# Attention with a mixture of experts on one core: grouping rewritten and shared with ScalarE and GpSimd, stacks of batch 0 ahead of most row stores, five unread products between the first scores

## Chip, cores, metric

One core of one Trainium2 chip. The metric is the device time of one execution in microseconds, median of several runs. One launch computes everything.

## What is computed

`x` has 8 batches of 512 tokens with 128 features, fp32. The reference, cut to what matters:

```python
xn = layernorm(x)                                   # no weights
q, k, v = xn @ Wq + bq, xn @ Wk + bk, xn @ Wv + bv  # 8 heads of 16
attn = softmax(q k^T / 4)
out = attn (v1 - lam v2)      # v1: first four heads' values, v2: last four, each used by both halves
s = (0.2 * (layernorm(out) * ln_w + ln_b)) @ Wo + bo
h = mod(int(xn[:, 0] + xn[:, 1]), 8)                # routing: experts h and h+1
f = sum over the two experts e of 0.5 * (relu(xn @ W1[e] + b1[e]) @ W2[e] + b2[e])
y = x + s * silu(f)
```

## The kernel before, in words

**Layout.** A batch is four tiles of 128 tokens, so there are 32 token tiles (`NT`). Attention takes 256 score products (`score` n, line 1289), one for each batch, head and query tile; VectorE takes the negative maximum of each (line 1049). 24 places later the same scores are made again with keys in the partitions and the maximum taken off (`exp` n, line 1314), ScalarE takes the exponential (line 787), and `pv` (line 1327) sums. To have fp32 scores from bf16 products, q and k are each split into three bf16 parts (`parts`), of which six pairs are stacked along the partitions of `qs` and `ks` by DMAs of SyncE. For batches 0 and 1 the split is done by peels: TensorE makes the projection again and subtracts the parts already there (lines 1255 and 1258), and ScalarE copies the rest out as the next part (line 774). For batch 1 the parts are in a piece of `probs`.

**Mixture.** The tokens are sorted by expert. VectorE computes h for each token (`count_groups`, lines 886 to 911): v01 = xn0 + xn1, its integer part towards zero, modulo 8; then `onehot`, `count` per expert and partition, and running sums `seen`. TensorE sums the counts over the partitions (`route` 1, lines 1359 and 1360), `make_slots` turns them into a slot for each token, `find_tokens` (lines 943 to 948) and `find_rows` (line 953) build bf16 indicator tiles, and 32 products (`invert`, line 1367) give `inverse`: which token stands in each sorted slot. GpSimd then gathers tiles of 128 sorted tokens from the DRAM copy `xn_rows` (line 650). It first waits for `inverse` and for all eight stores of that copy (line 541, SyncE). Seven extra tiles (f = 0 to 6) hold tokens at the edges between experts: `turn_tile`, `hidden`, `down`, then z (line 1167), stored by SyncE to `init_rows` (line 556). The 32 sorted tiles (f = 7 to 38) follow at one per 6.85 scores; each begins with a gather of `init_rows` (line 678) that waits for all stores of z, and VectorE adds its products to it (lines 1174, 1176).

**Order.** All engines walk one list, `schedule()`: every step has a time written by hand, the list is sorted by it, and each engine does its own kinds of steps in that order. The unit is one score; times below 0 are the head. Nothing but that order and the semaphores decides when a step runs. `ring` is three PSUM banks given in turn to transposes, projections, peels, route, invert and the expert products; a new user waits for the reader of the use three back.

**The head.** VectorE takes bn_stats of each batch as it lands (line 1005). GpSimd makes rstd = (var + eps) ** -0.5 (lines 630, 631) and shift = -mean * rstd (lines 629, 635), by groups of batches (`LN_GROUPS`); for the last group the shift is made by VectorE (line 1019). ScalarE normalises batches 0 to 3 (line 755), GpSimd 4 to 7 (line 640). TensorE waits for DVE's `count` at `route`, which stands behind all of batch 0's peels and batch 1's transpose. Both peels of each of batch 1's projections stand ahead of `invert`. ScalarE's list goes: norms, batch 0's parts, batch 1's transpose copy, norms 2 and 3 among batch 1's parts, bias copies (lines 743 to 747, which set `table_ready`, a condition of score 0), ten small loads (lines 718 to 727), the DMAs of ones (line 731), then tile 0's transpose copy (line 832). SyncE's list goes: stores of batches 0 and 1, twelve stack DMAs of batch 0 (line 532), stores of batches 2 to 7, the W2 loads (line 502, once tile 1 has landed), a store of b2, z of tile 0, then twelve stack DMAs of batch 1, stores of z, and pair loads.

## Time and profile before

| what | us |
|---|---|
| median of three runs (409.14 to 410.87) | 409.66 |
| the profiled execution | 411.52 |
| its span, first to last instruction | 409.6 |
| TensorE busy | 381.5 (93%) |
| VectorE busy | 291.8 (71%) |
| ScalarE busy | 267.5 (65%) |
| GpSimd busy | 189.3 (46%) |

The mean granted TensorE clock is 0.991 of full speed. In the profile PE is TensorE, PEld its weight loads, DVE is VectorE, ACT ScalarE, POOL GpSimd and SP SyncE; a q behind the name is the engine's queue, which issues DMAs. L12 is line 12 of the kernel. In the chain of waits each piece is what the next had to wait for.

### The profile page before, as it was taken

To read this page: it belongs to the slowest core of one execution; us is meant where nothing else is said; L and a number is where in the kernel's file an instruction comes from. 1 tells how busy PE (TensorE), PEld (TensorE's weight loads), DVE (VectorE), ACT (ScalarE), POOL (GpSimd) and SP (SyncE) were. 2 spreads that over 40 slices of the span, in tenths; PEclk is the share of its full clock that TensorE was granted. 3 is DMA by queue.
4 is the path that set the end of the run, shared out by engine and by line. 5 is a ranking of instruction groups with operands and counts; after the bars stand their busy time and mean duration, and the time that the engine had idled before them with its cause. 6 is when DMAs were issued, how large, how long until landed. Compare 5 with 4: busy or idle time off the path is not lost.

```text
span 409.6 us, 8427 instructions
## 1 busy us (share of the span) xinstructions
PE 381.5 (93%) x2576; PEld 248.3 (61%) x2576; DVE 291.8 (71%) x758; ACT 267.5 (65%) x667; POOL 189.3 (46%) x262
## 2 busy tenths in 40 slices
PE   4996989999999999999999999999999999999993
PEld 2353876565775667766665668765676667764321
DVE  7787996656686757766676767866686767866884
ACT  3581756666765776576666767676766668675783
POOL 7944203454456543565355532663573444541200
PEclk9996999999999999999999999999999999999999
DMA  7975953263216451265105640346136141216740
GB/s 263 343 230 112 242 196 91 80 206 105 79 37 191 111 195 21 79 190 168 46 27 170 189 140 18 136 121 197 48 127 216 22 169 47 81 26 213 230 159 26
DMA packets 36945, 54.75 MB, mean 134 GB/s; under 512 B 6724, under 2 KB 25141, under 8 KB 36903
## 3 DMA queue, kind: packets, MB, share of 16 engines
q1 hardware_dynamic: 31456, 46.94, 34.6%
q0 software_dynamic: 3296, 6.76, 7.8%
q10 hardware_dynamic: 2151, 0.53, 0.6%
q8 instruction: 22, 0.36, 0.4%
q14 instruction: 20, 0.16, 0.1%
HBM read 15.59 MB, written 6.75 MB: 55 GB/s over the span
## 4 chain that ended last, share of the span: by engine, by line
PE 74%; DVE 7%; DMA 5%; ACT 4%; SPq 4%; issue 4%; POOL 1%; ACTq 0%; DVEq 0%; POOLq 0%
PE ring L1393 14%; PE pv_bank L1327 13%; PE ring L1414 12%; PE score L1289 12%; PE exp L1314 10%; PE ring L1251 3%; DVE neg_max L1049 3%; DMA xs<-xn_rows,inverse 3%; SPq L532 2%; PE ring L1335 2%; PE ring L1255 1%; PE ring L1353 1%; PE ring L1276 1%; PE ring L1375 1%; PE score L1264 1%
## 5 line engine op out<-in xcount | busy, mean ns | idle before, releaser
L1049 DVE TENSOR_REDUCE neg_max<-score 128x1 f32<-128x512 f32 x256 | 169.0, 683 | 72.3 <-PE score L1289 66.7
L1289 PE MATMUL score<-ks,qs 96*128 96x512 bf16 x256 | 98.3, 386 | 6.3 <-DVE neg_max L1049 6.0
L787 ACT ACTIVATE probs<-exp 128x512 f32<-128x512 f32 x124 | 72.5, 605 | 36.3 <-PE exp L1314 32.3
L787 ACT ACTIVATE xin<-exp 128x512 f32<-128x512 f32 x120 | 69.7, 604 | 38.5 <-PE exp L1314 38.1
L1314 PE MATMUL exp<-qs,ks 99*128 99x512 bf16 x244 | 91.7, 380 | 0.1
L825 ACT ACTIVATE hT<-ring,pair 128x128 f32<-128x128 f32 x256 | 73.4, 377 | 13.0 <-PE ring L1393 11.9
L1414 PEld LDWEIGHTS ring<-w_sb,hT 128*128 128x128 f32 x568 | 73.5, 191 | 10.4 <-issue 3.5
L1414 PE MATMUL ring<-w_sb,hT 128*128 (+1 forms) x568 | 75.4, 275 | 0.9 <-ACT hT L825 0.9
L1393 PEld LDWEIGHTS ring<-xsT,pair 128*128 128x128 f32 x512 | 66.3, 191 | 14.6 <-issue 8.1
L1393 PE MATMUL ring<-xsT,pair 128*128 128x128 f32 x512 | 68.2, 276 | 1.7 <-issue 1.2
L684 POOL TENSOR_SCALAR tanh<-tanh 128x128 f32<-128x128 f32 x32 | 17.2, 536 | 95.5 <-ACT tanh L845 95.2
L1289 PEld LDWEIGHTS score<-ks,qs 96*128 96x128 bf16 x256 | 25.9, 102 | 45.3 <-DVE neg_max L1049 24.0
L650 POOL DMA_INDIRECT xs<-xn_rows,inverse x39 | 38.5, 988 | 24.3 <-issue 10.2
L678 POOL DMA_INDIRECT y_sb<-init_rows,init_row x32 | 31.2, 974 | 29.0 <-DMA init_rows<-oT 17.3
L691 POOL DMA_INDIRECT y_rows<-y_sb,inverse x32 | 34.4, 1076 | 9.0 <-POOL y_sb L685 9.0
L1327 PE MATMUL pv_bank<-xin,va 128*32 128x512 f32 x256 | 31.2, 599 | 0.8 <-ACT xin L787 0.7
L1314 PEld LDWEIGHTS exp<-qs,ks 99*128 99x128 bf16 x244 | 23.9, 98 | 12.5 <-issue 1.9
L1327 PE MATMUL pv_bank<-probs,va 128*32 128x512 f32 x256 | 31.2, 599 | 0.0
L1174 DVE SCALAR_TENSOR_TENSOR y_sb<-ring,first_expert,y_sb 128x128 f32<-128x128 f32 x32 | 11.1, 348 | 15.2 <-PE ring L1375 8.7
L1251 PE MATMUL ring<-xT,wqk 128*128 128x512 f32 x32 | 18.0, 657 | 1.3 <-ACT xT L750 1.3
L845 ACT ACTIVATE tanh<-y_sb 128x128 f32<-128x128 f32 x32 | 9.8, 305 | 11.2 <-DVE y_sb L1176 11.1
L769 ACT ACTIVATE parts<-ring,qk_bias 128x512 bf16<-128x512 f32 x14 | 9.6, 689 | 9.7 <-PE ring L1251 9.7
(198 smaller groups left out, 417.4 us busy)
## 6 DMA issues: line engine op xcount, KB each, us to landing
pair<-table SPq DMA_DIRECT2D x32, 580.0 KB
qs<-parts SPq DMA_DIRECT2D x42, 128.0 KB
ks<-parts SPq DMA_DIRECT2D x42, 128.0 KB
xin<-_attn_hidden_states_dram SPq DMA_DIRECT2D x8, 256.0 KB, 4.4
table<-in_L_ffn_W_dram SPq DMA_DIRECT2D x2, 1024.0 KB, 9.2
w_sb<-in_L_ffn_W_dram SPq DMA_DIRECT2D x8, 256.0 KB, 10.4
xn_rows<-xn SPq DMA_DIRECT2D x8, 256.0 KB, 3.0
table<-_attn_hidden_states_dram SPq DMA_DIRECT2D x8, 256.0 KB, 5.4
```

The lines of the kernel that those rows point to most:

```text
L650: pool.indirect_dma_start(xs[:, f % XS, :], None, xn_rows, bass.IndirectOffsetOnAxis(ap=inverse[:, f:f + 1], axis=0)).then_inc(tile_loaded ...
L678: pool.indirect_dma_start(y_sb[:, tile % YB, :], None, init_rows, bass.IndirectOffsetOnAxis(ap=init_row[:, tile:tile + 1], axis=0)).then_i ...
L691: pool.indirect_dma_start(y_rows, bass.IndirectOffsetOnAxis(ap=inverse[:, f:f + 1], axis=0), y_sb[:, tile % YB, :], None).then_inc(y_store ...
L787: a.activation(prob(n), exp_banks[n][:, :], ACT.Exp, scale=SCALE).then_inc(exp_done, 1)
L825: last = a.activation(hT[:, f % 2, FC * j + c, :], shared[:, c * P:(c + 1) * P], ACT.Relu, bias=bias)
L1049: v.tensor_reduce(neg_max[:, b % 2, col:col + 1], score_bank[n % 2][:, :], AX.X, ALU.max, negate=True).then_inc(max_taken, 1)
L1251: t.matmul(shared[:, :], wqk[:, i, :], xT[:, b % 2, :], start=True, stop=True).then_inc(shared_filled, 1)
L1289: t.matmul(score_bank[n % 2][:, :], qs[0:MAX_ROW, b % STK, hh, c * P:(c + 1) * P], ks[0:MAX_ROW, b % STK, hh, :], start=True, stop=True).t ...
L1314: t.matmul(exp_banks[n][:, :], ks[0:KROWS, b % STK, hh, kc * P:(kc + 1) * P], qs[0:KROWS, b % STK, hh, :], start=True, stop=True).then_inc ...
L1327: last = t.matmul(pv_bank[VW * i:VW * (i + 1), :], va[:, b % 2, kc, i, :], prob(4 * n4 + i), start=(kc == 0), stop=(kc == C - 1))
L1393: last = t.matmul(shared[:, c * P:(c + 1) * P], w1_chunk, xsT[:, f % 2, :], start=True, stop=True)
L1414: last = t.matmul(shared[:, half * D:(half + 1) * D], hT[:, f % 2, k, :], w2_chunk, start=(k % FC == 0), stop=(k % FC == FC - 1))
```

## The change

- Groups of batches: the last pair is split, (6, 7) and (7, 8). GpSimd makes no shift in the groups behind batch 3; it makes that of batches 4 to 7 at once behind the last `rstd`. VectorE's shift is gone: it adds -2 * mean to the sum of the two raw features before `rstd` is there, and multiplies by `rstd` after.
- `count_groups`: integers are read and written without casts between; `seen` is made by a scan over `onehot` shifted by one element.
- ScalarE makes the second of the two token products (`tokens`); ScalarE also normalises batch 4, and batch 2 earlier.
- `route` goes ahead of batch 0's last peel; the second peels of batch 1's two projections go behind score 1 and score 5.
- SyncE: batch 2's store goes ahead of batch 0's stacks, batch 0's last stack part behind the stores of 4, 5 and 6. The ones DMAs move from ScalarE's queue to SyncE's, ahead of W2.
- `keep_busy`: one unread product behind each of scores 2, 3 and 4 and two behind the peel that follows score 5, each 96x128 by 96x512 in bf16 into an unused bank.
- Extra tiles start one score later (`FFN_FIRST`), and small moves of tanh, `split_max` and the gathers of `init_rows` (`TANH`, `SPLIT_MAX`, `INIT_AHEAD`).

The diff, with its context cut:

```diff
-LN_GROUPS = ((0, 1), (1, 2), (2, 4), (4, 6), (6, 8))
-POOL_NORM = (4, 5, 6, 7)
+LN_GROUPS = ((0, 1), (1, 2), (2, 4), (4, 6), (6, 7), (7, 8))
+POOL_NORM = (5, 6, 7)
+LATE_SHIFT = 4
+EARLY_GROUPS = 3
 STATS_AT = (-60, -59, -58, -57, -56, -55, -54, -52)
-SHIFT_AT = (-58.5, -57.5, -55.5, -53.5, -50)
-NORM_AT = (-58, -56.4, -49.9, -47.93, -49.2, -49.1, -49, -48.95)
+SHIFT_AT = (-58.5, -57.5, -55.5, -53.5, -53.4, -50)
+NORM_AT = (-58, -56.4, -56.3, -48.61, -48.7, -48.68, -48.66, -48.63)
 FOLD_QK_AT = -57.95
-QKV_AT = (-57.9, -50, 35, 67, 99, 131, 163, 181)
+QKV_AT = (-57.9, -48.62, 35, 67, 99, 131, 163, 181)
 PROJECT_AT = ((-55.9, -55.6), (-47.95, -45.9))
-PEEL_AT = (((-55.5, -55.3), (-55.4, -55.25)), ((-45.5, -45.3), (-45.4, -45.2)))
-STACK_AT = (((-55.58, -55.45, -55.28), (-55.57, -55.35, -55.2)), ((12.1, 12.3, 12.5), (12.2, 12.4, 12.6)))
+PEEL_AT = (((-55.5, -55.3), (-55.4, -48.65)), ((-45.5, 1.5), (-45.4, 5.3)))
+STACK_AT = (((-55.58, -55.45, -55.28), (-55.57, -55.35, -48.64)), ((12.1, 12.3, 12.5), (12.2, 12.4, 12.6)))
 ROUTE_AT = (-48.8, -48.7)
-TOKENS_AT = -45
+TOKENS_AT = -45.6
 INVERT_AT = -40
-EXTRAS_AT = 5.2
-GROUPS_AT = (9.05, 10.72, 13.05, 14.05)
+EXTRAS_AT = 5.9
+GROUPS_AT = (9.05, 10.72, 12.55, 14.05)
 ONES_AT = -45.09
-FFN_FIRST = 7.6
+FFN_FIRST = 8.6
 FFN_PACE = 6.85
-TX, DX = 2.4, 3.2
+TX, DX = 3, 3.2
 PAIR_AT = (20, 21, 22)
-INIT_AHEAD = 1.5
+INIT_AHEAD = 1.67
 TT = 2
-SPLIT_MAX, TURN_MAX = 16.8, 18.9
+SPLIT_MAX, TURN_MAX = 16.5, 18.9
 FOLD_AT = 20.5
-TANH, GATE = 0.7, 1.84
+TANH, GATE = 1, 1.84
 HALVES = 2
+WARM_AT = ((2.5, 1), (3.5, 1), (4.5, 1), (5.4, 2))
...
     at(INVERT_AT, "invert")
+    for time, products in WARM_AT:
+        at(time, "keep_busy", products)
...
         sign = sb("sign", [P, NT])
-        h = sb("h", [P, NT])
+        h_i = sb("h_i", [P, NT], I32)
...
         inverse_f = cmp[:, 0:FT]
-        onehot = work[:, 512:768].rearrange("p (e t) -> p e t", e=EXP)
-        seen = work[:, 768:1024].rearrange("p (e t) -> p e t", e=EXP)
+        onehot = work[:, 511:767].rearrange("p (e t) -> p e t", e=EXP)
+        seen = work[:, 767:1023].rearrange("p (e t) -> p e t", e=EXP)
...
         token_ready = sem("token_ready")
+        in_tile_ready = sem("in_tile_ready")
...
                                          parts_of(b)[:, i, k, :]).then_inc(stacked[b % STK], 16)
+                elif kind == "ones":
+                    sp.wait_ge(dve_consts, 1)
+                    for slot_b in range(STK):
+                        sp.dma_start(ks[MAX_ROW:KROWS, slot_b, :, :],
+                                     ones_bf[:, :].unsqueeze(1).to_broadcast([PARTS, HEADS, S])).then_inc(ones_stacked, 16)
...
                     pool.wait_ge(stats_ready, end)
-                    if end < B:
+                    if first < LATE_SHIFT:
                                     ALU.pow).then_inc(rstd_ready, 1)
-                    if end < B:
+                    if first < LATE_SHIFT:
                         g.tensor_tensor(shift[:, tok], shift[:, tok], rstd[:, tok], ALU.mult).then_inc(shift_ready, 1)
+                    if end == B:
+                        late = slice(C * LATE_SHIFT, NT)
+                        pool.wait_ge(rstd_ready, len(LN_GROUPS))
+                        link(g.tensor_scalar(shift[:, late], mv[:, late, 0], -1.0, None, ALU.mult))
+                        g.tensor_tensor(shift[:, late], shift[:, late], rstd[:, late], ALU.mult).then_inc(shift_ready, 1)
+                        pool.wait_ge(shift_ready, EARLY_GROUPS + 1)
                     b = s[1]
-                    pool.wait_ge(shift_ready, 1 + [b >= end for _, end in LN_GROUPS].index(False))
...
                     act.dma_start(lnb_sb[:, :], ln_b.rearrange("(p a) -> p a", a=1)).then_inc(small_loaded, 16)
-                elif kind == "ones":
-                    act.wait_ge(dve_consts, 1)
-                    for slot_b in range(STK):
-                        act.dma_start(ks[MAX_ROW:KROWS, slot_b, :, :],
-                                     ones_bf[:, :].unsqueeze(1).to_broadcast([PARTS, HEADS, S])).then_inc(ones_stacked, 16)
...
                     a.activation(xT[:, s[1], :], shared[:, :], ACT.Copy).then_inc(xT_ready, 1)
+                elif kind == "tokens":
+                    act.wait_ge(in_tile_ready, 1)
+                    a.activation(token[:, 1, :, :, :], in_tile, ACT.Copy, scale=row_of[:, 0:1]).then_inc(token_ready, 1)
...
             v.memset(zeros, 0.0)
+            v.memset(work[:, 767:768], 0.0)
...
                 dve.wait_ge(pair_summed, 1)
+                dve.wait_ge(rstd_ready, len(LN_GROUPS))
                 link(v.tensor_tensor(v01[:, :], v01[:, :], rstd[:, :], ALU.mult))
-                dve.wait_ge(shift_ready, len(LN_GROUPS))
-                link(v.scalar_tensor_tensor(v01[:, :], shift[:, :], 2.0, v01[:, :], ALU.mult, ALU.add))
                 v.tensor_scalar(sign[:, :], v01[:, :], 0.0, 2.0, ALU.is_ge, ALU.mult)
-                link(v.tensor_copy(n_abs[:, :], whole_i))
-                link(v.tensor_tensor(over, n_abs[:, :], v_abs[:, :], ALU.is_gt))
-                link(v.tensor_tensor(n_abs[:, :], n_abs[:, :], over, ALU.subtract))
-                link(v.scalar_tensor_tensor(h[:, :], sign[:, :], -1.0, n_abs[:, :], ALU.add, ALU.mult))
-                link(v.tensor_copy(whole_i, h[:, :]))
-                link(v.tensor_scalar(whole_i, whole_i, EXP - 1, None, ALU.bitwise_and))
-                link(v.tensor_copy(h[:, :], whole_i))
-                link(v.tensor_tensor(onehot[:, :, :], h[:, :].unsqueeze(1).to_broadcast([P, EXP, NT]),
+                link(v.tensor_tensor(over, whole_i, v_abs[:, :], ALU.is_gt))
+                link(v.tensor_tensor(n_abs[:, :], whole_i, over, ALU.subtract))
+                link(v.scalar_tensor_tensor(h_i[:, :], sign[:, :], -1.0, n_abs[:, :], ALU.add, ALU.mult))
+                link(v.tensor_scalar(h_i[:, :], h_i[:, :], EXP - 1, None, ALU.bitwise_and))
+                link(v.tensor_tensor(onehot[:, :, :], h_i[:, :].unsqueeze(1).to_broadcast([P, EXP, NT]),
-                flat = work[:, 768:1024]
-                link(v.tensor_tensor_scan(flat, work[:, 512:768], zeros,
-                                          0.0, ALU.add, ALU.add))
-                v.tensor_tensor(seen[:, :, :], seen[:, :, :], onehot[:, :, :], ALU.subtract).then_inc(seen_ready, 1)
+                v.tensor_tensor_scan(work[:, 768:1024], work[:, 511:767], zeros,
+                                     0.0, ALU.add, ALU.add).then_inc(seen_ready, 1)
...
                 dve.wait_ge(slots_split, 1)
-                link(v.tensor_tensor(in_tile, by_pair(slot_tile[:, 0:NT], FT), over_pairs(columns[:, :, :], NT // 2), ALU.is_equal))
-                v.tensor_tensor(token[:, 0, :, :, :], in_tile, by_pair(ordinal[:, :], FT), ALU.mult)
-                v.tensor_scalar(token[:, 1, :, :, :], in_tile, row_of[:, 0:1], None, ALU.mult).then_inc(token_ready, 1)
+                v.tensor_tensor(in_tile, by_pair(slot_tile[:, 0:NT], FT), over_pairs(columns[:, :, :], NT // 2),
+                                ALU.is_equal).then_inc(in_tile_ready, 1)
+                dve.wait_ge(in_tile_ready, 1)
+                v.tensor_tensor(token[:, 0, :, :, :], in_tile, by_pair(ordinal[:, :], FT), ALU.mult).then_inc(token_ready, 1)
...
                         continue
-                    tok = slice(C * first, C * end)
-                    v.tensor_tensor(v01[:, :], xin[:, :, 0], xin[:, :, 1], ALU.add).then_inc(pair_summed, 1)
-                    dve.wait_ge(rstd_ready, g + 1)
+                    link(v.tensor_tensor(v01[:, :], xin[:, :, 0], xin[:, :, 1], ALU.add))
                     dve.wait_ge(stats_ready, end)
-                    v.scalar_tensor_tensor(shift[:, tok], mv[:, tok, 0], -1.0, rstd[:, tok],
-                                           ALU.mult, ALU.mult).then_inc(shift_ready, 1)
+                    v.scalar_tensor_tensor(v01[:, :], mv[:, :, 0], -2.0, v01[:, :],
+                                           ALU.mult, ALU.add).then_inc(pair_summed, 1)
...
                              ks[0:MAX_ROW, b % STK, hh, :], start=True, stop=True).then_inc(score_filled, 1)
+                elif kind == "keep_busy":
+                    for _ in range(s[1]):
+                        t.matmul(exp_bank[1][:, :], qs[0:MAX_ROW, 0, 0, 0:P], ks[0:MAX_ROW, 0, 0, :], start=True, stop=True)
...
                 elif kind == "invert":
-                    pe.wait_ge(token_ready, 1)
+                    pe.wait_ge(token_ready, 2)
```

## Rows read from the trace of the kernel before

**Rows 1.** Busy time by stretch: engines, granted clock, DMA share, GB/s.

```profile
29.00:30.00 1.00, 1.00 (x24) 0.88 (x23) 0.97 (x5) 0.78 (x2) 0.00 (x0) 1.00 0.00 0
...
34.00:35.00 1.00, 0.00 (x0) 0.00 (x0) 0.96 (x4) 0.00 (x0) 0.78 (x1) 0.50 0.42 115
...
100.00:150.00 50.00, 48.59 (x344) 33.26 (x343) 35.23 (x84) 34.24 (x87) 25.26 (x32) 1.00 0.38 116
```

**Rows 2.** Chain of waits to 75 us: start, us, what.

```profile
31.45 4.89 DMA xs<-xn_rows,inverse
...
37.93 1.71 PE ring L1393 x8
...
61.53 2.96 DMA init_rows<-oT
```

**Rows 3.** VectorE in order of time, scores: start, us, line, [idle before, releaser].

```profile
31.06 3.67 DVE L1049 TENSOR_REDUCE neg_max<-score 128x1 f32<-128x512 f32 x6
...
37.39 1.29 DVE L1049 TENSOR_REDUCE neg_max<-score 128x1 f32<-128x512 f32 x2 [1.16 <-PE score L1289]
...
40.10 1.29 DVE L1049 TENSOR_REDUCE neg_max<-score 128x1 f32<-128x512 f32 x2 [1.42 <-PE score L1289]
...
43.78 0.35 DVE L1167 SCALAR_TENSOR_TENSOR oT<-ring,uses_extra,oT 128x128 f32<-128x128 f32 x1
...
68.92 0.35 DVE L1174 SCALAR_TENSOR_TENSOR y_sb<-ring,first_expert,y_sb 128x128 f32<-128x128 f32 x1 [1.21 <-DMA y_sb<-init_rows,init_row]
```

**Rows 4.** GpSimd in order of time: powers, shift and norms.

```profile
8.14 1.04 POOL L631 TENSOR_TENSOR rstd<-var_eps,neg_half 128x4 f32<-128x4 f32 x1
...
14.60 0.20 POOL L635 TENSOR_TENSOR shift<-shift,rstd 128x8 f32<-128x8 f32 x1
...
15.21 1.67 POOL L631 TENSOR_TENSOR rstd<-var_eps,neg_half 128x8 f32<-128x8 f32 x1
...
16.87 8.19 POOL L640 TENSOR_SCALAR xn<-xin,rstd,shift 128x128 f32<-128x128 f32 x16
```

**Rows 5.** VectorE in order of time: the grouping.

```profile
16.91 0.17 DVE L1019 SCALAR_TENSOR_TENSOR shift<-mv,rstd 128x8 f32<-128x8 f32 x1 [2.00 <-POOL rstd L631]
...
17.21 0.19 DVE L892 SCALAR_TENSOR_TENSOR v<-shift,v 128x32 f32<-128x32 f32 x1
...
17.98 0.28 DVE L897 CAST n_abs<-hT 128x32 f32<-128x32 int32 x1
...
18.98 0.18 DVE L901 CAST hT<-h 128x32 int32<-128x32 f32 x1
...
21.22 0.49 DVE L911 TENSOR_TENSOR hT<-hT 128x256 f32<-128x256 f32 x1
...
26.79 0.54 DVE L948 TENSOR_SCALAR probs<-hT,row_of 128x1248 bf16<-128x1248 bf16 x1
...
27.24 2.42 DVE L953 TENSOR_TENSOR qs<-hT,grid 128x1536 bf16<-128x1536 bf16 x3
```

**Rows 6.** Costliest groups of the page: busy us, mean ns.

```profile
L787 ACT ACTIVATE probs<-exp 128x512 f32<-128x512 f32 x124 | 72.5, 605 | 36.3 <-PE exp L1314 32.3
...
L825 ACT ACTIVATE hT<-ring,pair 128x128 f32<-128x128 f32 x256 | 73.4, 377 | 13.0 <-PE ring L1393 11.9
```

**Rows 7.** ScalarE in order of time: a norm, loads issued, ones, tile copy.

```profile
21.94 1.64 ACT L755 ACTIVATE xn<-xin,shift,rstd 128x128 f32<-128x128 f32 x4
...
29.33 0.35 ACTq L718 DMA_DIRECT2D lams<-in_L_attn_lambda_q_dram  x1
...
34.46 2.46 ACTq L731 DMA_DIRECT2D ks<-ones_bf  x3
...
36.97 0.28 ACT L832 ACTIVATE xsT<-ring 128x128 f32<-128x128 f32 x1 [6.96 <-PE ring L1375]
```

**Rows 8.** TensorE in order of time: a late peel of batch 1.

```profile
27.83 1.02 PE L1255 MATMUL ring<-xT,wqk 128*128 128x512 f32 x2
```

**Rows 9.** Stores of normalised rows, line 541: time to landing.

```profile
DMA to landing us min/median/max: 2.1/3.0/8.1
```

## The prediction

> **What bounds the kernel now.** I read the stretches first. From 100 us on TensorE is busy 48.6 of 50 us [rows 1], and the stretches after it look alike until the drain. A head start won in front of that region is therefore passed on to the end unless something else sets its beginning. So the question is when the dense region begins. The chain of waits says what leads there: the grouping on VectorE, the gather of the first tile of sorted tokens (31.45 to 36.34), the products of that tile, then from 44 us SyncE issuing DMAs one after another, the last store of `init_rows` (61.53 to 64.49), its gather, and VectorE waiting 1.21 us for it at 68.92 [rows 2, 3]. The reader should see three things in it. (a) Everything up to 31.15 us is latency: `inverse` ends there and the gather's issue starts 0.3 us later. (b) TensorE is idle from 34 to 36.4 us, and its granted clock falls to 0.50, the 1.2 GHz level, as the last of six scores, with 0.2 us of idle time between each two, is through; the eight products of the first tile then take 1.71 us, and would take half of that at 2.4 GHz [rows 1, 2]. (c) VectorE waits for TensorE twice there, 1.16 us before the score maximum at 37.39 and 1.42 us before the one at 40.10 [rows 3].
>
> **The routing chain on VectorE.** It waits for `rstd` of the last group, done by GpSimd at 16.88. GpSimd is the late one: its powers follow each other. The new split makes two powers of 4 columns (1.04 us each) out of one of 8 (1.67 us), and one more var_eps (0.3 us from its start to the power's): 0.7 us longer. The two shift operations taken out of the group of batches 4 and 5 (the second 14.60 to 14.88) give back 0.6 us [rows 4]. So `rstd` comes at 16.9 to 17.1, and this edit buys nothing; I take 16.9. Behind it five dependent operations go: the shift added to v01 (0.19), three casts (0.28, 0.18, 0.18 for the one not shown) and the subtraction in `seen` (0.49), 1.32 us, with the shift's 0.08 us of start-to-start time: 1.4 us [rows 5]. Added are the wait-free -2·mean term (hidden in the 2.0 us wait for `rstd`) and nothing else. Moving the route products ahead of the last peel of batch 0 is needed for this, since that peel held TensorE until 20.85. Then the product of `in_tile` with the row number leaves VectorE: 26.79 to 27.24, another 0.45 us [rows 5]. Rows now end at 29.58, and would end at 27.7: 1.85 us earlier.
>
> **That product on ScalarE.** It has no row. The nearest: 377 ns for 128 elements with a bias per row (L825) and 605 ns for the 512 of an exp without (L787) [rows 6], about 0.6 ns per element; against the 280 ns of a tile copy (36.97) it is 0.85 [rows 7]. From a norm (0.41 us for 128 elements, 1.64 for four) 1248 elements then cost 1.1 to 1.4 us. Bounds: 0.45 us as on VectorE, and 2.5 us at twice the slope. I take 1.3: the tile copy and the exp are alike in form and differ in length alone. ScalarE also gains batch 4's norms (1.64 us) and does batch 2's earlier; by my list of its work in order it reaches the token product at 25.5 and ends it at 26.8, ahead of the last rows at 27.7. So it is hidden; at 2.5 us it would end at 28.0 and cost 0.1 to 0.3 us. GpSimd keeps 12 of 16 norms (8.19 us for 16): from about 17.5, behind the late shift, to 23.7 [rows 4].
>
> **Inversion and gather.** The two last peels of batch 1 (1.02 us of fp32 products each and one or two bf16 ones of 0.2 us behind them) leave the stretch before the inversion [rows 8], and the inversion waits for the rows alone: 28.1 instead of 30.6, `inverse` at 28.65 instead of 31.15, gather landed at 33.85 instead of 36.34 with the old 4.89 us [rows 2]. First maximum: `table_ready` comes at about 28.5 behind ScalarE's bias copies, so 29.05 instead of 31.06 [rows 3], 2.0 us.
>
> **Between the first scores.** The two peels put in take 1.3 us of TensorE each. The first delays score 2 by half a microsecond on VectorE; the rest stands in gaps of 0.2 us and in the old idle time. The five products nobody reads cost 0.22 us each, 1.1 us, all in time in which TensorE waited for maxima or the gather; with the cover gone they would cost 1.1 us. TensorE is then busy from 29 to within half a microsecond of tile 0, so I expect 1.00 granted throughout. It saves about half of the products in 36.4 to 40.6 (1.71 becomes 0.86 for tile 0) [rows 2]. With that, and hidden 0 one score later, VectorE's two waits (2.6 us [rows 3]) shrink to 0.8 us, 0.45 behind the first peel and 0.35 behind hidden 0.
>
> **ScalarE before tile 0.** The three ones DMAs (2.46 us of its queue) go to SyncE, which is idle there. But the ten small loads (29.33 to 34.46, where the ones DMAs follow) now stand ahead of the last two peels [rows 7]. They start with the third copy of batch 1, about 28.45, and end at 33.55; two copies of 0.6 us follow; tile 0 is copied at 34.75 to 35.05, instead of 36.97. So 1.9 us there, and late is not the gather but ScalarE. Counting on: maximum 8 done at 36.6, hidden 0 ends at 36.6, groups 0 at 38.4, groups 1 at 40.0, maximum 11, then z of tile 0 at 40.9 instead of 44.13 [rows 3]: 3.2 us. VectorE's own work is 3.7 us ahead there, as z now follows maximum 11.
>
> **SyncE and init_rows.** From z of tile 0 the queue runs without a gap: 12 stack DMAs, stores, pairs, until the transfer that starts at 61.53 [rows 2]. It moves rigidly by 3.2 us. The last z comes one score, a tile copy and two bias operations later (about 1.4 us), at 57.9 with VectorE's 3.7 us; SyncE reaches its store at 58.3 and still is the late one. `y_sb` is there at 65.7 instead of 68.92. Behind this TensorE's and VectorE's orders are the same. Only the tanh moves on ScalarE behind one exp or copy in 11 of 32 tiles, 0.6 us each; the tile's store and the gather two tiles on follow it a whole tile (some 9 us) ahead of their use. GpSimd's order stays. Zero; with that cover gone, 0.6 us a tile.
>
> **Sum:** 2.0 (first maximum) + 1.8 (VectorE's waits, 2.6 less 0.8) - 0.6 (a maximum of that length now ahead of z) = 3.2 us, carried on by SyncE. The profiled execution took 411.52 us (span 409.6 us), so 408.3 us; it stands 1.9 us over the median of 409.66 us, and against that median the forecast is **406.4 us**. Bounds of its own: 2.2 us if the gather or ScalarE is 1 us later, 4.2 us if they are earlier: 405.5 to 407.5.
>
> **A rule that speaks against it.** GpSimd's norms average 0.51 us (8.19 for 16) and run beside VectorE's chain [rows 4]. The Trainium skill (SBUF — State Buffer, section on its two separate sides) says that a VectorE operation with two SBUF inputs and a GpSimd operation hold a shared port pair one at a time. This trace agrees as far as the norms go: some take 0.8 us, others 0.45.
>
> **Rivals.** Port: what leaves the chain are mostly one-input casts; seven operations with two SBUF inputs stay beside the norms. If each now meets a norm at a worse moment, half of one, 0.25 us, is added: 1.7 us of the 3.2, 407.9 us. That is what the skill's rule would allow; for it speaks the spread of the norms, against it that VectorE had the same neighbour before. ScalarE: if its list before tile 0 is 1.5 us longer than counted (the token product at its upper bound, loads issued late), 1.7 us remain, 408.0 us. For it: 5.1 us of issues in a row. More: if SyncE's chain no longer leads, VectorE's 3.7 us plus the 1.2 us wait at 68.92 come through, 4.9 us at most, 404.8 us. Little: the clock falls all the same, VectorE's 1.8 us are not won, and its last z, 1.4 us later in the order, comes at 59.7 with the store's transfer at 60.4; 1.1 us is left, 408.6 us. For it: the products nobody reads fill the gaps only in part. Slower: the gather also waits for all eight stores of normalised rows. They take 3.0 us in the median and 8.1 us at worst to land [rows 9], and the one of batch 3 is now last, issued at about 25.4. Landing after 31.4 it decides; at 8.1 us it lands at 33.5, 2.1 us later than the gather's start today, TensorE cools again, and the time is 411.8 us. Against it: no DMA moves from 29 to 30 us today [rows 1], and the bytes are the same.
>
> **How the numbers follow.** Chances: forecast 0.56, port 0.08, ScalarE 0.12, more 0.12, little 0.08, slower 0.04. A measurement tells about 0.5%, 2.05 us, from no change. Faster takes the forecast, more and about half of the port and ScalarE cases: 0.78; slower 0.04; the rest, 0.18, is the same. The range takes in the forecast, the middle cases and most of more: 404.7 to 408.9 us.
>
> **What would show it.** Right: v_abs about 0.25 us behind `rstd`, `count` near 19.6, `inverse` near 28.7, granted clock 1.00 from 30 to 44 us, tile 0 copied by ScalarE near 35, z of tile 0 near 41, `y_sb` near 65.7, and the same distance from there to the end. Wrong: the clock at 0.5 before tile 0 although the products are there, the gather released by the stores, or a dense region that begins 3 us earlier and ends where it did.

## The result and the profile after

| | median, us | range, us | runs |
|---|---|---|---|
| before, in this comparison | 410.57 | 409.04 to 411.90 | 20 |
| after | 409.01 | 406.57 to 414.18 | 20 |

The ratio is 0.9965 (95%: 0.9948 to 0.9981), 0.35% or 1.4 us faster, where 3.2 us were forecast. The forecast's median, 406.4 us, lies below every one of the 20 runs of after; the fastest comes within 0.2 us of it. Of the 2.6 us between that forecast and the median, 0.9 us lie in its starting point: before's three runs had a median of 409.66 us, its twenty here one of 410.57. The rest is what has to be explained. The second thing to see is the width: the runs of before lie within 2.9 us, those of after within 7.6 us.

The profiled execution of after took 409.53 us (span 407.8, mean granted clock 0.995), 2.0 us under the 411.52 us of before's.

Stretches of after: busy time of TensorE, its weight loads, VectorE, ScalarE, GpSimd, then the granted clock, DMA share, GB/s.

```profile
29.00:30.00 1.00, 0.68 (x15) 0.53 (x12) 0.32 (x2) 1.00 (x5) 0.00 (x0) 1.00 0.18 30
34.00:35.00 1.00, 1.00 (x5) 0.39 (x4) 0.93 (x4) 0.16 (x1) 0.11 (x1) 1.00 0.24 61
...
68.00:70.00 2.00, 1.59 (x9) 0.95 (x8) 1.90 (x8) 1.27 (x3) 1.03 (x2) 0.88 0.24 25
70.00:72.00 2.00, 2.00 (x11) 1.15 (x13) 1.48 (x4) 1.00 (x5) 1.58 (x2) 0.50 0.13 39
72.00:74.00 2.00, 2.00 (x17) 0.38 (x10) 0.00 (x0) 0.31 (x2) 0.76 (x2) 0.76 0.16 41
...
100.00:150.00 50.00, 49.17 (x350) 33.92 (x348) 35.90 (x84) 34.16 (x87) 25.77 (x33) 1.00 0.39 118
```

Against [rows 1] the hole at 34 us is gone (TensorE busy 1.00 of 1, clock 1.00). But there is a new one: from 70 to 72 us the granted clock is 0.50, the 1.2 GHz level, in a place where before had none.

TensorE of after in order of time: the first bias products, then the transpose of tile 8, its eight products, and an attention step.

```profile
6.72 3.75 PE L1272 MATMUL score<-probs,ones 2*128 2x512 f32 x4 [6.72 <-DMA probs<-in_L_ffn_b_dram]
...
67.75 0.33 PE L1386 MATMUL ring<-ident,xs 128*128 128x128 f32 x1 [1.25 <-DMA xs<-xn_rows,inverse]
...
69.37 1.76 PE L1404 MATMUL ring<-xsT,pair 128*128 128x128 f32 x8
...
71.29 2.72 PE L1338 MATMUL pv_bank<-probs,va 128*32 128x512 f32 x16
```

TensorE waits 1.25 us for tile 8's gathered tokens. Before it waited 0.58 us there. Within two microseconds, while it is busy again, it runs at half the clock: by the chain (next fence) tile 8's eight products take 1.60 us where tile 0's take 0.89.

Chain of waits of after, as in [rows 2].

```profile
31.92 4.97 DMA xs<-xn_rows,inverse
...
37.50 0.89 PE ring L1404 x8
...
60.66 2.33 DMA init_rows<-oT
...
63.76 3.75 DMA y_sb<-init_rows,init_row
...
69.53 1.60 PE ring L1404 x8
```

VectorE of after in order of time, as in [rows 3, 5]; in square brackets the idle time before it and who ended it.

```profile
19.13 0.42 DVE L917 TENSOR_REDUCE count<-hT 128x8 f32<-128x256 f32 x1
...
21.09 0.17 DVE L925 TENSOR_TENSOR_SCAN group_end<-ring,hT 128x8 f32<-128x8 f32 x1 [0.88 <-PE ring L1371]
...
26.19 2.42 DVE L963 TENSOR_TENSOR qs<-hT,grid 128x1536 bf16<-128x1536 bf16 x3
...
29.92 0.18 DVE L1149 CAST inverse<-hT 128x39 int32<-128x39 f32 x1
...
30.27 1.29 DVE L1057 TENSOR_REDUCE neg_max<-score 128x1 f32<-128x512 f32 x2 [0.17 <-PE score L1297]
32.00 2.48 DVE L1057 TENSOR_REDUCE neg_max<-score 128x1 f32<-128x512 f32 x4 [0.44 <-PE score L1297]
...
36.36 1.89 DVE L1057 TENSOR_REDUCE neg_max<-score 128x1 f32<-128x512 f32 x3 [0.39 <-PE score L1297]
38.65 0.69 DVE L1057 TENSOR_REDUCE neg_max<-score 128x1 f32<-128x512 f32 x1 [0.40 <-PE score L1297]
...
42.31 0.34 DVE L1175 SCALAR_TENSOR_TENSOR oT<-ring,uses_extra,oT 128x128 f32<-128x128 f32 x1
...
67.53 0.35 DVE L1182 SCALAR_TENSOR_TENSOR y_sb<-ring,first_expert,y_sb 128x128 f32<-128x128 f32 x1 [1.86 <-DMA y_sb<-init_rows,init_row]
...
80.16 0.34 DVE L1182 SCALAR_TENSOR_TENSOR y_sb<-ring,first_expert,y_sb 128x128 f32<-128x128 f32 x1
```

The second `y_sb` of before:

```profile
79.98 0.34 DVE L1174 SCALAR_TENSOR_TENSOR y_sb<-ring,first_expert,y_sb 128x128 f32<-128x128 f32 x1
```

ScalarE of after in order of time, as in [rows 7]: the token product, the first and the last small load, tile 0's copy.

```profile
26.68 1.32 ACT L764 ACTIVATE probs<-hT,row_of 128x1248 bf16<-128x1248 bf16 x1
...
28.25 0.35 ACTq L734 DMA_DIRECT2D lams<-in_L_attn_lambda_q_dram  x1
...
33.41 1.38 ACTq L743 DMA_DIRECT2D lnb_sb<-in_L_attn_ln_b_dram  x1
...
36.08 0.28 ACT L846 ACTIVATE xsT<-ring 128x128 f32<-128x128 f32 x1
```

The steps, in us from the start, with two experiments beside them (e1 and e8, below):

| | before | forecast | after | e1 | e8 |
|---|---|---|---|---|---|
| first bias products start | 5.82 | - | 6.72 | 5.85 | 6.05 |
| `count` ends | 20.51 | 19.6 | 19.55 | 19.47 | 19.58 |
| `inverse` ends | 31.15 | 28.65 | 30.10 | 29.05 | 29.48 |
| first maximum starts | 31.06 | 29.05 | 30.27 | 28.99 | 29.55 |
| z of tile 0 ends | 44.13 | 40.9 | 42.65 | 41.63 | 41.90 |
| first `y_sb` (tile 7) | 68.92 | 65.7 | 67.53 | 66.28 | 66.04 |
| second `y_sb` (tile 8) | 79.98 | - | 80.16 | 77.34 | 77.17 |

The last row is the finding. After leads by 1.39 us at the first `y_sb` and trails by 0.18 us one tile later: between the two it takes 12.63 us, before 11.06 us. The stretch at half clock costs 1.57 us and eats the lead. From the second `y_sb` to that of the last tile it takes 291.71 us in after (until 371.87) and 293.74 us in before (until 373.72), with the granted clock at 1.00 in both. The change doesn't explain those 2.0 us: e7 below keeps before's order and takes 291.70 us for that distance. So the 2.0 us by which the profiled execution of after beats before's come from a stretch in which the change gains nothing. That is one more reason not to read the change's worth from one pair of executions.

### The profile page after: what moved, and what is told of

It is laid out like the page before. It is cut to its first block, busy times and chain, and to the rows that moved or that the text cites. A ratio compares the mean times of both kernels' runs of the same rounds, so it can differ in the third digit from the quotient of the medians.

```text
span 407.8 us, 8433 instructions
## 1 busy us (share of the span) xinstructions
PE 381.6 (94%) x2580; PEld 248.3 (61%) x2581; DVE 290.8 (71%) x753; ACT 269.5 (66%) x672; POOL 187.9 (46%) x260
## 4 chain that ended last, share of the span: by engine, by line
PE 78%; DVE 7%; DMA 5%; issue 3%; ACT 3%; SPq 2%; POOL 1%; ACTq 0%; DVEq 0%; POOLq 0%
PE pv_bank L1338 14%; PE ring L1404 13%; PE ring L1425 13%; PE score L1297 12%; PE exp L1325 10%; PE ring L1259 4%; DVE neg_max L1057 3%; DMA xs<-xn_rows,inverse 2%; PE ring L1346 2%; PE ring L1364 1%; PE ring L1263 1%; PE ring L1284 1%; DMA probs<-in_L_ffn_b_dram 1%; PE ring L1386 1%; DMA y_sb<-init_rows,init_row 1%
## 5 line engine op out<-in xcount | busy, mean ns | idle before, releaser
L1297 PE MATMUL score<-ks,qs 96*128 96x512 bf16 x256 | 97.3, 382 | 5.1 <-DVE neg_max L1057 4.3
L1338 PEld LDWEIGHTS pv_bank<-xin,va 128*32 128x32 f32 x256 | 6.5, 109 | 15.6 <-issue 10.3
L701 POOL TENSOR_TENSOR y_sb<-tanh,y_sb 128x128 f32<-128x128 f32 x32 | 14.6, 456 | 2.7
```

Source lines behind the costliest of these rows:

```text
L1297: t.matmul(score_bank[n % 2][:, :], qs[0:MAX_ROW, b % STK, hh, c * P:(c + 1) * P], ks[0:MAX_ROW, b % STK, hh, :], start=True, stop=True).t ...
L1338: last = t.matmul(pv_bank[VW * i:VW * (i + 1), :], va[:, b % 2, kc, i, :], prob(4 * n4 + i), start=(kc == 0), stop=(kc == C - 1))
```

## The experiments

All compute the whole output; some add products that nobody reads. They ran in three groups (e1 to e4, e5 to e8, e9 to e12), each on a chip of its own with its own runs of before (medians 410.40, 409.99 and 410.06 us); ratios are against those, with their 95% interval.

**e1: are the five unread products what holds the clock before tile 0?**

```diff
-WARM_AT = ((2.5, 1), (3.5, 1), (4.5, 1), (5.4, 2))
+WARM_AT = ()
```

> The changed kernel without its five unread products (nothing else). Theory clock: TensorE is idle in gaps between scores again, its granted clock falls to 0.50 before tile 0 as in the kernel before, the first products of tile 0 take about 1.7 us instead of 0.9 and the time is 1 to 1.6 us longer than the changed kernel's. Rival: the two peels between the scores keep the clock up by themselves, the clock stays at 1.00 from 30 to 44 us, and the time is that of the changed kernel within 0.5 us.

408.21 us (406.73 to 410.10, 12 runs), ratio 0.9959 (0.9939 to 0.9979). Stretches of e1, then TensorE's transpose of tile 0:

```profile
34.00:36.00 2.00, 1.09 (x4) 0.40 (x4) 1.26 (x7) 0.79 (x3) 0.40 (x1) 1.00 0.44 112
...
70.00:72.00 2.00, 2.00 (x18) 0.91 (x11) 0.58 (x3) 0.35 (x2) 1.44 (x2) 1.00 0.17 53
```

```profile
34.69 0.33 PE L1386 MATMUL ring<-ident,xs 128*128 128x128 f32 x1 [0.94 <-DMA xs<-xn_rows,inverse]
```

The clock stays at 1.00 before tile 0 without them, with TensorE idle for nearly half of 34 to 36 us, so the five products aren't what holds it. What is left against before are the two peels between the scores and a shorter wait for tile 0's tokens, 0.94 us against 2.40; no run separates these two. Its time and after's can't be told apart. By chance its profiled execution also shows the forecast's head: bias products at 5.85, `inverse` at 29.05, no fall at 70 us, 406.73 us.

**e2: gather tile 8 ahead of the `init_rows` gather.** Tile 8's gather stands behind that one on GpSimd, which waits for the last store of z.

```diff
-        at(t - 6.66, "load_x", f)
+        at(25.4 if f == NX + 1 else t - 6.66, "load_x", f)
```

> The changed kernel with one gather moved: GpSimd gathers the tokens of tile 8 ahead of the first gather of init_rows, which waits for the stores of z. Theory second gap: in the changed kernel TensorE waits 1.25 us for tile 8 at 67.8 us and its clock then falls until about 74 us (1.76 us for eight products, 2.7 us for sixteen sums); with tile 8 there, TensorE's gap shrinks to the wait for a maximum, the clock stays at 1.00 and the time falls by 1.5 to 2.5 us against the changed kernel, with less scatter. Rival: VectorE waits for the gather of init_rows all the same (1.9 us), holds the score maxima and so TensorE, the clock falls as before and the time is the same within 0.5 us.

409.05 us (407.48 to 410.22), ratio 0.9971 (0.9953 to 0.9988). TensorE of e2 at that place:

```profile
67.81 0.39 PE L1297 MATMUL score<-ks,qs 96*128 96x512 bf16 x1 [1.30 <-DVE neg_max L1057]
```

The gap has the same length with another releaser: the score in front waits for VectorE, which itself waited for the `init_rows` gather. TensorE's hole is that gather's lateness, whoever is named at its end.

**e3: the two bias products later, behind `count`.** Meant to show that the head's late start at 6.72 us matters.

```diff
-BIAS_AT = -58.2
+BIAS_AT = -48.3
```

> The changed kernel with the bias products (line 1272, which wait for the b2 rows from DRAM at the head of TensorE's list and took 3.75 us) moved behind batch 1's transpose. Theory head: batch 0's transpose starts with its norm at about 9.2 us instead of 10.5, its parts come 1.3 us earlier, route is not held, VectorE's 0.88 us wait at 21.09 goes, inverse is ready at 28.7 to 29.3 instead of 30.1, and the time falls by 0.5 to 1.2 us. Rival: the products are needed to raise the clock; without them the projections and peels stay at the 1.2 GHz level longer and inverse is not earlier than 30.1.

409.37 us (407.78 to 412.47), ratio 0.9974 (0.9954 to 0.9995). The head did start without them (first transpose at 9.27 instead of 10.45 us), but the execution was one in which the clock fell elsewhere. TensorE and stretches of e3:

```profile
19.47 0.39 PE L1370 MATMUL ring<-count,before 128*128 128x8 f32 x2 [1.45 <-DVE count L917]
```

```profile
24.00:26.00 2.00, 2.00 (x3) 0.56 (x2) 1.97 (x3) 0.86 (x3) 0.00 (x0) 0.50 1.06 387
...
28.00:30.00 2.00, 2.00 (x4) 0.71 (x3) 0.18 (x2) 0.69 (x1) 0.00 (x0) 0.50 0.14 30
```

A gap of 1.45 us, then 0.50 from 21 to 31 us with TensorE busy 2.00 of 2; `inverse` came at 34.77. That one execution is the slowest of its twelve, 3.1 us over their median, so the median doesn't contain such a fall in most of them.

**e4: the old casts.** After, with before's casts and the subtraction in `seen`.

```diff
-                link(v.tensor_tensor(over, whole_i, v_abs[:, :], ALU.is_gt))
+                link(v.tensor_copy(n_abs[:, :], whole_i))
+                link(v.tensor_tensor(over, n_abs[:, :], v_abs[:, :], ALU.is_gt))
...
-                v.tensor_tensor_scan(work[:, 768:1024], work[:, 511:767], zeros,
-                                     0.0, ALU.add, ALU.add).then_inc(seen_ready, 1)
+                link(v.tensor_tensor_scan(flat, work[:, 512:768], zeros,
+                                          0.0, ALU.add, ALU.add))
+                v.tensor_tensor(seen[:, :, :], seen[:, :, :], onehot[:, :, :], ALU.subtract).then_inc(seen_ready, 1)
```

> The changed kernel with the integer section of the grouping put back: casts between integers and floats and the subtraction in seen (four more dependent VectorE operations, about 1.1 us). Theory head: VectorE had 0.88 us of waiting for TensorE's route products in front of make_slots, so only the rest passes: inverse 0.2 to 0.5 us later than 30.1, time within 0.5 us of the changed kernel. Rival (forecast): every dependent operation counts, inverse 1.1 us later and the time 1 us longer.

408.18 us (407.13 to 411.98), ratio 0.9958 (0.9937 to 0.9979): no slower than after. `count` ends at 20.12, as forecast, yet `inverse` at 29.74. The median against after's would say that the shorter chain buys nothing. Its profile shows another fall at tile 8, behind a gap of 1.67 us:

```profile
68.05 0.33 PE L1390 MATMUL ring<-ident,xs 128*128 128x128 f32 x1 [1.67 <-DMA xs<-xn_rows,inverse]
...
69.69 1.62 PE L1408 MATMUL ring<-xsT,pair 128*128 128x128 f32 x8
```

So the theory became: whether the clock falls differs from execution to execution, and that hides what the schedule is worth. A first look at it needs no new run, since the mean granted clock is on record for every execution. Where it is 0.999 or 1.000, e1's five executions have a median of 407.40 us and e4's eight one of 407.97: with hardly any half-clock time on either side, on one chip, the old casts cost 0.6 us (e4 also has the five unread products, which e1 lacks). The next runs fill the gaps.

**e5: two pair loads later on SyncE**, behind the last store of z.

```diff
-PAIR_AT = (20, 21, 22)
+PAIR_AT = (20, 26, 26.1)
```

> The changed kernel with SyncE's second and third pair loads moved behind the last two stores of z (they are used more than 10 us later). Theory chain: SyncE is what sets the gather of init_rows; the last z is ready at 59.15 and its store goes out at 60.66; without the pair loads in front, y_sb is there 1.0 to 1.5 us earlier after z of tile 0 (23.2 to 23.8 us instead of 24.7 to 24.9), TensorE's gap in front of tile 8 (1.0 to 1.7 us) goes or halves, the clock no longer falls at 66 to 74 us, and the time falls by 1 to 2 us against the changed kernel. Rival: the last z itself is the late one, nothing moves, same time within 0.5 us.

406.78 us (406.21 to 407.61, 6 runs), ratio 0.9924 (0.9910 to 0.9937). SyncE of e1, then of e5, and VectorE of e5:

```profile
57.84 0.52 SPq L577 DMA_DIRECT2D pair<-table  x1
58.40 1.54 SPq L567 DMA_DIRECT2D init_rows<-oT  x2
```

```profile
55.70 2.75 SPq L567 DMA_DIRECT2D init_rows<-oT  x2
...
59.60 1.77 SPq L577 DMA_DIRECT2D pair<-table  x2
```

```profile
65.12 0.35 DVE L1182 SCALAR_TENSOR_TENSOR y_sb<-ring,first_expert,y_sb 128x128 f32<-128x128 f32 x1 [0.49 <-PE ring L1425]
```

From z of tile 0 to the first `y_sb` it takes 23.53 us instead of 24.65 (e1) or 24.88 (after), and VectorE no longer waits for the gather. This confirms the forecast's picture of SyncE's chain, and the gap before tile 8 is a little smaller (0.89 us against e1's 1.01) and the runs are narrow (1.4 us).

**e6: the bias rows loaded ahead of Wq and Wk** on ScalarE's queue (two lines moved behind them).

```diff
-            act.dma_start(wq_sb[:, :], wq).then_inc(qk_loaded, 16)
-            act.dma_start(wk_sb[:, :], wk).then_inc(qk_loaded, 16)
...
             act.dma_start(b1_rows[:, :], b1.rearrange("e (c p) -> (e c) p", p=P)).then_inc(b1_loaded, 16)
+            act.dma_start(wq_sb[:, :], wq).then_inc(qk_loaded, 16)
+            act.dma_start(wk_sb[:, :], wk).then_inc(qk_loaded, 16)
```

> The changed kernel with the loads of b2 and b1 issued ahead of Wq and Wk on ScalarE's queue (0.85 us earlier). Theory head: the bias products at the head of TensorE's list start at about 5 us instead of 5.7 to 6.7, so batch 0's transpose starts with its norm (9.2), inverse is ready at 28.7 to 29.0 whatever DRAM does, and the time is 0.5 to 1 us shorter than the changed kernel's. Rival: landing is set by the traffic of the x loads and not by the issue, the products start at 5.7 to 6.7 as before and nothing changes.

408.63 us (407.29 to 412.53, 12 runs), ratio 0.9974 (0.9952 to 0.9997). The bias products start at 4.28 us, the transpose at 9.18, and `inverse` comes at 28.97, 0.08 us ahead of e1's. An early landing gains next to nothing; a late one (after's 6.72) costs 1 us.

**e7: before, with unread products** after the first scores, one, one, one and eight of them.

```diff
+WARM_AT = ((2.5, 1), (3.5, 1), (4.5, 1), (5.15, 8))
...
+    for time, products in WARM_AT:
+        at(time, "keep_busy", products)
```

> The kernel BEFORE with unread products alone: one behind each of scores 2, 3 and 4, eight ahead of tile 0's transpose (11 of 0.22 us, in 3.2 us of idle time). Theory clock: the granted clock stays at 1.00 from 30 to 44 us, tile 0's eight products take 0.9 us instead of 1.7, and the time falls by 1 to 2 us against the kernel before. Rival: VectorE and the gather set the pace there, the clock stays up and the time is that of before within 0.5 us.

409.17 us (407.79 to 410.73, 12 runs), ratio 0.9979 (0.9965 to 0.9993). Stretch and VectorE of e7:

```profile
36.00:38.00 2.00, 2.00 (x14) 1.32 (x14) 1.31 (x3) 0.62 (x3) 0.94 (x1) 1.00 0.23 46
```

```profile
67.20 0.35 DVE L1177 SCALAR_TENSOR_TENSOR y_sb<-ring,first_expert,y_sb 128x128 f32<-128x128 f32 x1 [1.44 <-DMA y_sb<-init_rows,init_row]
```

The clock stays at 1.00 at tile 0, and `y_sb` comes 1.72 us earlier than in [rows 3], with no change to the grouping. The median gains only 0.8 us, though, and it isn't the clock that keeps it there: seven of the twelve executions have a mean granted clock of 0.999 or 1.000, and their median is 409.28 us.

**e8: after, with more products nobody reads** where TensorE waits: six at each of two places of the grouping, four ahead of tile 0, six near 42 us, twelve ahead of tile 8.

```diff
+FILL_AT = ((-48.81, 6), (-48.3, 6), (5.45, 4), (12.9, 6), (32.1, 12))
...
+                elif kind == "fill":
+                    pe.wait_ge(iota_ready, 1)
+                    for _ in range(s[1]):
+                        t.matmul(pv_bank[:, 0:2 * P], ident_bf[:, :], grid[:, :, :].rearrange("p n i -> p (n i)"),
+                                 start=True, stop=True)
```

> The changed kernel with further unread products (0.11 us each, into a bank that nobody uses yet) in all of TensorE's longer gaps up to 70 us: 6 ahead of route, 6 ahead of batch 1's projections, 4 ahead of tile 0, 6 ahead of score 13, 12 ahead of tile 8. Theory scatter: the 7 us between the fastest and slowest runs of the changed kernel come from the clock, which falls in one of these gaps in some executions and costs 1.5 to 4.5 us; filled, the clock is 1.00 from 17 us to the tail, the runs lie within 2.5 us of each other and the median falls to 407 to 407.5. Rival: the scatter comes from DMA landings and not from the clock: scatter and median stay (408.2 to 409).

406.79 us (406.51 to 407.07, 5 runs), ratio 0.9919 (0.9906 to 0.9932). TensorE of e8 ahead of tile 8:

```profile
65.66 1.47 PE L1305 MATMUL pv_bank<-grid,ident_bf 128*128 128x256 bf16 x12
66.97 0.27 PE L1394 MATMUL ring<-ident,xs 128*128 128x128 f32 x1
...
67.95 1.05 PE L1412 MATMUL ring<-xsT,pair 128*128 128x128 f32 x8
```

By the ratios that is 0.46% or 1.9 us better than after, with intervals apart, and the spread is 0.6 us (5 runs) against 7.6 us (20 runs).

**e9: before (e7) with fillers** in the grouping and ahead of tile 8, `FILL_AT = ((-48.75, 4), (32.1, 12))`.

> The kernel BEFORE with unread products in its gaps: the 11 of the run before, 4 ahead of route and 12 ahead of tile 8. It prices the change with the clock held in both: the changed kernel so filled took 406.8 us. Theory (clock and schedule are two gains): the filled kernel before has little scatter and a median of 407.8 to 408.8 us, so that 1 to 2 us of the change are its shorter grouping and its order, and 1.5 to 2.5 us the clock. Rival: all of it is the clock, and the filled kernel before takes 406.5 to 407.3 us.

408.33 us (407.52 to 408.92, 6 runs), ratio 0.9952 (0.9937 to 0.9967). That is 1.1 us by the ratios below e7, most of whose executions had the clock held already, so part of what these fillers gain isn't explained by the granted clock. The two ratios come from different chips and their intervals just touch.

**e10: e8 with the old casts** (the diffs of e8 and e4 together).

> The changed kernel with its gaps filled and the integer section of the grouping put back (casts and subtraction, about 1.1 us of dependent VectorE work). Theory: with the clock held the delay shows, 0.5 to 0.9 us over 406.8, so 407.3 to 407.7 us; inverse 0.6 to 0.9 us later than in the filled kernel. Rival: the grouping isn't what gates the gather and the time is 406.8 within 0.3 us.

408.14 us (407.66 to 409.93, 9 runs), ratio 0.9957 (0.9943 to 0.9971), 1.35 us over e8 by the medians and 1.6 us by the ratios. The slowest of e8's five runs (407.07) is below the fastest of these nine. `inverse` of e8, then of e10:

```profile
29.30 0.18 DVE L1152 CAST inverse<-hT 128x39 int32<-128x39 f32 x1
```

```profile
29.67 0.18 DVE L1156 CAST inverse<-hT 128x39 int32<-128x39 f32 x1
```

Only 0.37 us of those stand in these two profiles at `inverse`, and 0.20 us at `y_sb` (66.24 against 66.04). The casts end later as forecast (`count` 20.23 against 19.58); why the medians lie further apart than the profiles is open. e8 and e10 ran on different chips. On one chip, e11 below (fewer fillers, new casts) is 0.56 us faster than e10 by the medians, close to the 0.6 us of e1 and e4; so 0.6 us is the better supported price of the casts, and it lies within the 0.5 to 0.9 us expected.

**e11: after with the filler ahead of tile 8 alone**, `FILL_AT = ((32.1, 12),)`.

> The changed kernel with only the 12 unread products ahead of tile 8 (the gap at 66 us). Theory (second gap): this gap alone lets the clock fall in most executions in which it falls; with it filled the median is 406.8 to 407.6 us and the scatter under 2 us. Rival: the earlier gaps (route, batch 1's projections, score 13) are as bad; the median stays at 408 to 409 us with runs over 410.

407.58 us (406.77 to 407.80, 5 runs), ratio 0.9935 (0.9919 to 0.9951): by the ratios 1.2 of the 1.9 us that all fillers gain over after, though its interval just touches after's, and a spread of 1.0 us.

**e12: e5, e6 and e8 together**, with eight products instead of twelve ahead of tile 8.

> The changed kernel with three things together: SyncE's pair loads behind the last stores of z, b2 and b1 loaded first on ScalarE's queue, and the gaps filled (8 ahead of tile 8 here). Theory: the gains of the pair loads (y_sb 1.2 us earlier) stand on top of the held clock: 405.3 to 406.2 us, little scatter. Rival: the pair loads helped only by closing the gap, so that it is 406.5 to 406.9 us as either alone.

406.05 us (405.40 to 406.46, 4 runs), ratio 0.9895 (0.9877 to 0.9912): 1.05% faster than before, the best of all, though its interval still touches e8's. The rival, that the pair loads help only by closing the gap, had 406.5 to 406.9 us. VectorE of e12:

```profile
65.26 0.35 DVE L1185 SCALAR_TENSOR_TENSOR y_sb<-ring,first_expert,y_sb 128x128 f32<-128x128 f32 x1 [0.49 <-PE ring L1433]
```

## Why the prediction was wrong

**The grouping chain: right.** `count` at 19.55 us (forecast 19.6). The token product on ScalarE took 1.32 us (forecast 1.3) and was hidden. SyncE moved rigidly: 24.79 us from z of tile 0 to `y_sb` before, 24.88 after. No row store held the gather (they landed in 2.6 to 7.6 us), and GpSimd's port cost nothing to be seen. Behind tile 8 the two orders are equally long, tanh moves included: 291.70 us to the last tile in e1 and in e7.

**The first maximum (term of 2.0 us): right in e1 (2.07), 0.8 us in the profiled execution.** There the bias rows landed 0.9 us later, TensorE's whole head began late, and VectorE waited 0.88 us for `route` at 21.09, a wait that the forecast had at zero. The forecast took the landing of a load from one execution and gave it no spread.

**VectorE's waits (1.8 us, less 0.6): 0.7 us.** Its three waits make 1.23 us (forecast 0.8), since TensorE hands it a score late three times: behind the first peel (0.44), behind tile 0's transpose, which waits for the gathered tokens (0.39), and behind tile 0's eight products (0.40). And 1.35 less 0.6 is what stands between first maximum and z: 13.07 us before, 12.38 after. Together 1.5 us at z of tile 0, where 3.2 were forecast.

**What tile 0 waits for: wrong, and small.** The forecast had "late is not the gather but ScalarE". In e1, whose head is the forecast's, the gather landed at 34.64 (forecast 33.85), TensorE's transpose waited 0.94 us for it, and ScalarE had been idle for 0.58 us when it copied the tile at 35.05. `inverse` came 0.4 us late and the gather took 5.18 us instead of 4.89; these 0.7 us are what z of tile 0 lacks there (41.63 instead of 40.9).

**The step that failed** is "Behind this TensorE's and VectorE's orders are the same", from which a head start of 3.2 us was carried to the end unchanged. "So I expect 1.00 granted throughout" held up to tile 0 (34 to 35 us: 1.00), but the clock was priced up to 44 us only. The work between tile 0 and tile 8 became shorter or moved forward, but SyncE's chain stayed as long as it was, so TensorE reached tile 8 with 1.25 us of nothing to do instead of 0.58. The forecast saw that gather as the late one and counted the wait as free. It isn't: in the profiled execution the clock fell behind it and took 1.57 us; e4, with the same fall, took 12.62 us between the two tiles where after took 12.63, and e1, e2, e3, e6 and e11, without a fall there, 11.05 or 11.06. So in that execution the forecast's 3.2 us shrank by 1.2 us at the first maximum, by 0.5 in VectorE's waits, by 0.1 on the way to the first `y_sb` and by 1.57 at tile 8. The late bias rows behind the 1.2 us don't explain the median: in e6 they land early, and its ratio (0.9974) is no better than after's. The "little" rival named the right cause, the clock, at the wrong place: tile 0, where the clock holds and the five products buy nothing (e1).

**How much is that in the median?** The profile shows one execution of each kernel, so for the others this is an inference, from four sides.

- With the gap at tile 8 filled and nothing else, after gains 1.2 us by the ratios (e11); with all gaps filled 1.9 us, and its runs lie within 0.6 us (e8).
- In the profiled executions of after's order the clock either fell ahead of the drain (after 409.53, e4 410.75, e3 412.47 us) or held until the drain (e1 406.73, e2 407.50, e5 406.21, e6 408.50, e8 406.99, e10 407.94, e11 406.95, e12 406.46).
- The mean granted clock of every execution is on record. The six of after's twenty at 0.991 or below took 410.17 to 414.18 us, the two at 0.999 took 407.36 and 407.93. e1's four at 0.990 or below took 409.60 to 410.10 us, its five at 0.999 or above 406.73 to 407.55: 2.9 to 3.7 us below before's median, which is the forecast's gain. In between the mean says little, because a fall in the drain alone gives 0.993 too (e2, 407.50 us) and the fall at tile 8 gave 0.995.
- Filled on both sides, before takes 408.33 us (e9, ratio 0.9952) and after 406.79 (e8, 0.9919), on two chips whose runs of before agree within 0.1 us.

So the new schedule is worth 1.4 us by the ratios if e8 is taken for it, and 0.7 us if e11 is, which ran on e9's chip with fewer fillers. The shorter casts are about 0.6 us of it (e4 against e1, e10 against e11). The fillers give before 2.0 us (one less e9's ratio, of 410 us) and after 1.9. The forecast was that after would win both, 3.2 us: that is what e8 does (3.3).

The clock isn't all of the scatter. e3 has an execution of 409.84 us at 1.000, e4 one of 409.02 at 1.000, and e7's seven at 0.999 or 1.000 lie between 407.81 and 409.58. The distance from the second `y_sb` to the last is 291.66 to 292.38 us in twelve profiled executions, but 292.75 in e6 and 293.74 in before, all at a granted clock of 1.00. In before one piece of that is a wait of 0.58 us for gathered tokens at 129.00 us, which e7 doesn't have. What sets these delays, and whether the fillers act on them too, is open. So is in which gap the clock falls in each unprofiled execution.

## What to carry to other kernels

When a latency chain gets shorter, go through the timeline of TensorE behind it and ask where it will now arrive early: each new idle microsecond can cost half-speed work behind it, and whether it does differs from execution to execution, so run many, look at the spread before reading a median, and sort the executions by their mean granted clock. Filling such a gap with products that nobody reads is cheap (1.47 us of them ahead of tile 8 left the two tiles 11.06 us apart in e11, and 11.28 in e9, in whose order the gap is shorter: 0.84 us in e7, 1.01 in e1). Moving what the waited-for transfer queues behind (two pair loads, e5) shortens the chain itself and gave as much as all fillers did.

## What was not expected of the hardware

- The granted clock fell to 0.50 after single gaps of 1.25, 1.45 and 1.67 us (after, e3, e4) and held after gaps of 1.01, 1.30 and 1.42 us (e1, e2, e6) and after one of 1.41 us ahead of `route` in e4. Length of the gap alone doesn't decide it.
- The fall comes late: in after the gap ends at 67.75 us and the clock is at 0.50 from 70 to 72 us, with TensorE busy all through those two. In e3 the gap ends at 19.47 and the clock stood at 0.50 from 21 to 31 us, about 10 us of full work.
- A DMA's landing differs between executions by as much as 1 us: the bias rows let TensorE start between 5.74 and 6.72 us in after, e1, e2, e4 and e5, which issue them alike.
